# Two conditioned linear layers in fp32 on one core: y's parts from PSUM in the first batch, W0's last slabs turned by VectorE, x and these slabs loaded as eight and four row blocks

## The reference

```python
def _L0_cond_ref(hidden_states, W, b, coeff, mask):
    output = jnp.einsum('bsi,oi->bso', hidden_states, W) + b
    sign = (2 * mask - 1).astype(hidden_states.dtype)
    diff = jnp.einsum('bsi,bio->bso', hidden_states, sign)
    return output + diff * coeff[:, None, None]

def _L1_cond_ref(x, adapter_ids, base_weight, base_bias, lora_A_w, lora_B_w):
    result = jnp.einsum('bsd,od->bso', x, base_weight) + base_bias
    A = lora_A_w[adapter_ids]
    Bw = lora_B_w[adapter_ids]
    h = jnp.einsum('bsd,brd->bsr', x, A)
    lora_out = jnp.einsum('bsr,bor->bso', h, Bw)
    return result + lora_out

x = x + _L0_cond_ref(x, W0, b0, coeff, mask)
x = x + _L1_cond_ref(x, ids, W1, b1, lora_a, lora_b)
```

## Time and profile before

| what | value |
|---|---|
| runs | 408.07, 409.04, 409.2 us; median 409.04 |
| the profiled execution | 409.28 us, its span 407.5 us |
| busy of the span | PE 98%, PEld 90%, DVE 71%, ACT 45%, POOL 7% |
| granted clock of PE | full in all 40 slices |
| moved | 63.33 MB in 93488 packets, mean 155 GB/s |
| issue to landing, median | mask 4.7 us, a quarter of x 6.3 us, slab of W0 5.3 us, of W1 7.7 us |

### The profile page before, as it was taken

How to read it: one execution, slowest core, us unless ns; L and a number is a source line. 1 busy time by engine, 2 the same in 40 slices (tenths; PEclk the granted TensorE clock), 3 DMA queues, 4 the chain that set the end, 5 groups by cost and what they waited for, 6 DMA issues and landing times.

```text
span 407.5 us, 6136 instructions
## 1 busy us (share of the span) xinstructions
PE 397.8 (98%) x2356; PEld 365.3 (90%) x2356; DVE 290.6 (71%) x375; ACT 183.2 (45%) x289; POOL 26.5 (7%) x43
## 2 busy tenths in 40 slices
PE   7999989999999999999999999999999999999995
PEld 5788878889999999999999999999999999999995
DVE  2578878866887688676887679675887679775523
ACT  3565645544435344354444444354345434353322
POOL 1234510000001000010001000010001000000000
PEclk9999999999999999999999999999999999999999
DMA  7999997159532892249622893339732693346002
GB/s 267 287 272 262 246 275 189 51 144 251 161 97 74 194 244 76 80 136 238 182 82 72 197 225 97 93 120 196 189 110 77 184 238 103 104 129 168 0 2 103
DMA packets 93488, 63.33 MB, mean 155 GB/s; under 512 B 3595, under 2 KB 90643, under 8 KB 93460
## 3 DMA queue, kind: packets, MB, share of 16 engines
q1 hardware_dynamic: 93298, 62.77, 59.2%
q10 hardware_dynamic: 162, 0.18, 0.1%
HBM read 51.39 MB, written 8.39 MB: 147 GB/s over the span
## 4 chain that ended last, share of the span: by engine, by line
PE 90%; DMA 5%; SPq 3%; issue 1%; DVE 1%; ACT 0%
PE ps L946 28%; PE ps L948 14%; PE ps L997 13%; PE ps L996 13%; PE ps L995 13%; PE ps L919 3%; DMA xraw<-in_x_dram 2%; PE ps L1018 2%; DMA xrows<-in_x_dram 2%; SPq L292 1%; PE ps L975 1%; PE ps L974 1%; PE ps L973 1%; DMA araw<-in_L_cond_lora_A_w_dram 1%; SPq L261 0%
## 5 line engine op out<-in xcount | busy, mean ns | idle before, releaser
L946 PE MATMUL ps<-xhl,whi 128*128 128x512 f32 x512 | 183.9, 397 | 0.1
L948 PE MATMUL ps<-xhl,wlo 128*128 128x256 f32 x512 | 143.2, 280 | 0.0
L946 PEld LDWEIGHTS ps<-xhl,whi 128*128 128x128 f32 x512 | 96.1, 188 | 19.6 <-issue 0.5
L997 PE MATMUL ps<-w1hi,yhl 128*128 128x344 f32 (+1 forms) x336 | 107.8, 321 | 0.0
L996 PE MATMUL ps<-w1lo,yhl 128*128 128x344 f32 (+1 forms) x336 | 107.6, 320 | 0.0
L995 PE MATMUL ps<-w1hi,yhl 128*128 128x344 f32 (+1 forms) x336 | 107.5, 320 | 0.0
L948 PEld LDWEIGHTS ps<-xhl,wlo 128*128 128x128 f32 x512 | 96.6, 189 | 0.4
L707 DVE SCALAR_TENSOR_TENSOR wlo<-wm,cs_minus,whi 128x1024 fp32r<-128x1024 f32 x62 | 80.0, 1291 | 20.7 <-ACT whi L487 20.7
L487 ACT ACTIVATE whi<-wm,cs_minus 128x1024 fp32r<-128x1024 f32 x62 | 71.5, 1153 | 39.7 <-DVE wm L700 39.7
L700 DVE SCALAR_TENSOR_TENSOR wm<-wm,cs_twice,w0t 128x1024 f32<-128x1024 int32 x62 | 80.1, 1291 | 3.9 <-DMA wm<-in_mask_Bx4096x_ik_dram 2.8
L527 ACT ACTIVATE ysum<-ps,b0col 128x256 f32<-128x256 f32 x64 | 30.4, 475 | 87.2 <-PE ps L948 87.0
(11 more groups left out here) (72 smaller groups left out, 234.2 us busy)
## 6 DMA issues: line engine op xcount, KB each, us to landing
wm<-in_mask_Bx4096x_ik_dram SPq DMA_DIRECT2D x64, 512.0 KB, 4.7
xraw<-in_x_dram SPq DMA_DIRECT2D x28, 256.0 KB, 6.3
w0raw<-in_L_cond_W_dram SPq DMA_DIRECT2D x8, 512.0 KB, 5.3
w1raw<-_L_cond_base_weight_dram SPq DMA_DIRECT2D x8, 512.0 KB, 7.7
out_dram<-zst SPq DMA_DIRECT2D x18, 172.0 KB, 2.0
bt<-bhl SPq DMA_DIRECT2D x48, 64.0 KB, 2.4
out_dram<-zst SPq DMA_DIRECT2D x8, 164.0 KB, 2.0
out_dram<-zst SPq DMA_DIRECT2D x7, 176.0 KB, 2.0
```

The source lines that it names most:

```text
L946: nc.tensor.matmul(ps[:, bank, :], whi[:, s, k, :], xhl[:, b % 2, k, :], start=(k == 0), stop=False, skip_group_check=True)
L948: op = nc.tensor.matmul(ps[:, bank, 0:S], wlo[:, s, k, :], xhl[:, b % 2, k, 0:S], start=False, stop=(k == KT - 1), skip_group_check=True)
L997: op = nc.tensor.matmul(dst, lo, w1hi[:, c, cols], start=False, stop=(c == KT - 1), skip_group_check=True)
```

## The change

**(a) y in the first batch.** For n < 8 `layer1` becomes `first_layer1`: whi x xhi, whi x xlo and wlo x xhi are three matmuls of 256 columns that all add into the same 256 columns of PSUM. So `half_y` and `make_y` fall away there; `first_y_hi` (ACT) and `first_y_lo` (DVE, one scalar_tensor_tensor) read PSUM directly. yhl has three places in this part. Layer 1 of the next chunk waits for `first_y_lo`.

**(b) W0's slabs 5, 6 and 7** are loaded by four DMAs each into the layout that x has, and DVE turns them, `turn_w0`, in place of two units on PE and two copies on ACT each. POOL adds the unit matrix in that layout in one operation.

**(c) `load_x`**, for all batches, is eight DMAs of 128 partitions by 256 elements, one per block of 32 rows, in place of four.

**(d) The order of stage 1** is written anew on all engines. **(e)** `HELD` has one tile more.

```diff
+    W0D = range(5, KT)
-    HELD = ((1, 2),)
+    HELD = ((1, 1), (1, 2))
...
-                for a in range(4):
-                    src = x[b, :, a * S:(a + 1) * S].rearrange("(n q) f -> q n f", q=Q)
-                    sp.dma_start(xraw[a * Q:(a + 1) * Q, :, :], src).then_inc(x_in, 16)
+                for r in range(S // Q):
+                    src = x[b, r * Q:(r + 1) * Q, :].rearrange("q (a f) -> a q f", f=S)
+                    sp.dma_start(xraw[:, r, :], src).then_inc(x_in, 16)
...
+                if c in W0D:
+                    for r in range(P // Q):
+                        src = W0[c * P + r * Q:c * P + (r + 1) * Q, :].rearrange("q (a f) -> a q f", f=S)
+                        sp.dma_start(w0raw[:, s, r * S:(r + 1) * S], src).then_inc(w0_in[c], 16)
+                else:
+                    sp.dma_start(w0raw[:, s, :], W0[c * P:(c + 1) * P, :]).then_inc(w0_in[c], 16)
...
+            def first_y_hi(n):
+                act.wait_ge(l1_done, n + 1)
...
+                nc.scalar.activation(yhl[:, n % 3, 0:S], ps[:, l1_bank(n), 0:S], ACT.Identity,
+                                     bias=b0col[:, n:n + 1]).then_inc(y_hi, 1)
...
+            def turn_w0(c):
+                dve.wait_ge(w0_eyed, c + 1)
+                nc.vector.transpose(w0t[:, c, :, :].rearrange("p k (n q) -> p n k q", q=Q),
+                                    w0raw[:, c % W0S, :].rearrange("p (n i k) -> p n k i", n=4, k=KT)).then_inc(w0_by_dve, 1)
...
+            def first_y_lo(n):
+                dve.wait_ge(y_hi, n + 1)
+                nc.vector.scalar_tensor_tensor(yhl[:, n % 3, S:2 * S], ps[:, l1_bank(n), 0:S], b0col[:, n:n + 1],
+                                               yhl[:, n % 3, 0:S].bitcast(F32), ALU.add, ALU.subtract).then_inc(y_lo, 1)
...
+                    if not low:
+                        nc.tensor.matmul(ps[:, l1_bank(n), 0:S], whi[:, s, k, :], xhl[:, 0, k, 0:S],
+                                         start=(k == 0), stop=False, skip_group_check=True)
+                    if low is not False:
+                        op = nc.tensor.matmul(ps[:, l1_bank(n), 0:S], whi[:, s, k, :], xhl[:, 0, k, S:],
+                                              start=False, stop=(low is True and k == KT - 1), skip_group_check=True)
+                    if not low:
+                        op = nc.tensor.matmul(ps[:, l1_bank(n), 0:S], wlo[:, s, k, :], xhl[:, 0, k, 0:S],
+                                              start=False, stop=(low is None and k == KT - 1), skip_group_check=True)
```

More of the change, by code:

```diff
@@ L506, in rows_hi @@
                 if b == 1 and g == 1:
-                    act.wait_ge(unit_turned, max(number["w0", 5, 1], number["b", 0, 1]) + 1)
-                elif b == 1:
-                    act.wait_ge(unit_turned, number["w0", KT - 1, 1] + 1)
+                    act.wait_ge(unit_turned, number["b", 0, 1] + 1)
+                if b == 1:
+                    for c in (5,) if g == 1 else (6, 7):
+                        if c in W0D:
+                            act.wait_ge(w0_by_dve, c - W0D.start + 1)
+                        else:
+                            act.wait_ge(unit_turned, number["w0", c, 1] + 1)
                 if b >= 2:
@@ L696, in make_w @@
                 dve.wait_ge(mask_in[n % MS], 16 * (n // MS + 1))
-                if b == 0:
+                if b == 0 and c in W0D:
+                    dve.wait_ge(w0_by_dve, c - W0D.start + 1)
+                elif b == 0:
                     dve.wait_ge(w0_copied, 2 * (c + 1))
@@ L814, in _ @@
             split_lo("w1", 2, 1)
+            chunk_lo(3)
             split_lo("a", 0, 0)
             split_lo("a", 0, 1)
-            chunk_lo(3)
-            make_y(2)
+            first_y_lo(2)
+            turn_w0(5)
             make_w(4)
@@ L920, in turn_unit, with first_layer1 @@
                 op.then_inc(unit_turned, 1)
-            def layer1(n, ks):
-                b, c = divmod(n, KT)
-                bank = l1_bank(n)
+            def first_layer1(n, ks, low=None):
                 s = n % WS
-                if ks[0] == 0:
+                if ks[0] == 0 and not low:
                     if n < 2:
@@ L938, in layer1 @@
+                if ks[-1] == KT - 1 and low is not False:
+                    op.then_inc(l1_done, 1)
+            def layer1(n, ks):
+                b, c = divmod(n, KT)
+                bank = l1_bank(n)
+                s = n % WS
+                if ks[0] == 0:
+                    pe.wait_ge(w_lo, n + 1)
+                    if n == KT:
+                        pe.wait_ge(y_lo, KT)
+                    elif n == KT + 1:
                         pe.wait_ge(parts_lo, parted(number["w1", KT - 1, 0]))
-                    if c == 0 and b > 0:
+                    else:
+                        pe.wait_ge(y_made, n - 1 - KT)
+                    if c == 0:
@@ L1125, in _ @@
-            layer1(6, range(6, 8))
-            first_layer2(4, 1, 1)
-            adapter_h(5)
+            first_layer1(5, range(2, 4))
+            first_layer1(5, range(4, 6))
+            first_layer1(5, range(6, 8))
+            first_layer2(3, 1, 1)
+            first_layer2(4, 0, 0)
+            first_layer2(4, 1, 0)
+            adapter_h(4)
+            first_layer2(4, 0, 1)
+            first_layer1(6, range(0, 2))
+            first_layer1(6, range(2, 4))
+            first_layer1(6, range(4, 6))
@@ L1143, in _ @@
+            turn_unit("w1", 7, 0)
+            first_layer2(6, 1, 1)
+            turn_unit("w1", 7, 1)
+            adapter_h(7)
             layer1(8, range(0, 2))
```

328 lines of the change are left out of this document (156 added, 172 removed).

## The result

The changed kernel takes 458.96 us (456.75 to 459.58, 4 runs) against 409.12 us for the kernel before: 1.121 times as long, 95% interval 1.117 to 1.126. The profiled execution took 458.37 us, its span is 456.6 us, 49.1 more than before.

The account below looks back on a forecast made before the run. The prediction took PE, busy 98% of 407.5 us, as the bound, but expected the transfers to decide: 16.8 + 24.0 - 0.2 = +40.6 on the profiled 409.28, about 450 us, range 418 to 485.

Parts of the forecast that it names:

- four engines: The new x and W0 slab loads run on 4 of 16 DMA engines, their source's first count; chance 0.82.
- (a): Rival: all 16 DMA engines share the new loads as before; -3.6, 405.4 us, faster; chance 0.12.
- (b): Rival: four engines, and x's own price of 74 ns per 1 KB piece stays; about 505 us; chance 0.06.
- (c): Rival: 16 engines, but the 64 added weight loads on PE show, +13.8; 419 us; chance 0.04.
- (d): Rival: the parts cancel within 1.2 us, DVE's three turns making PE wait as long as it saves; chance 0.02.
- The engines' part: Gain with transfers at no cost: -2.64 for PE's removed transposes, -0.8 at the start, -0.2 at the end; -3.6 us.
- The price, 48 ns: Time for 1 KB on one DMA engine in the new loads; 12.3 us for x, 6.1 for a W0 slab.
- Each later batch, 4.0: x lands late, so PE waits 4.0 us for wlo in each of six batches, x(2) to x(7): +24.0.
- (e): Rival: with four engines PE waits 5 to 9 us at a time and runs slower afterwards; 6 more, 456 us.
- the factor of 1.6: PE work after a long wait takes up to 1.6 times as long, over some 10 us.
- Stage 1, +16.8: x(1) lands at about 80.2, not 53.3, so chunk 9's layer 1 begins at 100.0, not 83.23; bounds +8 and +26.
- Lie inside that wait and count nothing: Stage 1: the engines' gains there are hidden in PE's wait for the late loads and add 0.

Follow-up runs that it names:

- the 16-partition run: The changed kernel with W0's slabs in the 32-partition shape and x in eight DMAs of 16 partitions by 8 by 256: 413.41 us, ratio 1.006.

## Why the prediction was right, and where its terms were off

The forecast was 450 us for 458.96, by four engines, which was given 0.82, and the rivals fell: (a) 405.4 is what the same change takes when the loads do use 16 engines (405.78 measured); (b) fell with the price of a piece; (c) with the kernel of both old loads at 405.78, not 419; (d) with it.

- **The engines' part**, -3.6: measured -3.9 (405.78 against 409.64), and -4.7 with x in eight DMAs. Right in sum. The end's -0.2 is hardly seen (about 0.1), in stage 1 there is a little more. The -2.64 for the transposes and the -0.8 for the start were not tried one by one. The 64 added weight loads show in PE's timeline of the changed kernel:

```profile
63.22 0.28 PE L973 MATMUL ps<-xhl,whi 128*128 128x256 f32 x1
63.34 0.28 PE L976 MATMUL ps<-xhl,whi 128*128 128x256 f32 x1
63.46 0.28 PE L979 MATMUL ps<-xhl,wlo 128*128 128x256 f32 x1
63.58 0.40 PE L1026 MATMUL ps<-w1hi,yhl 128*128 128x512 f32 x1
```

Three products of 256 columns take 63.58 - 63.22 = 0.36, where 0.352 was the pace before: 64 x 0.008 = 0.5 us, near the 0 that was taken and far from 13.8.
- **Four engines**: share 0.27 and 96 GB/s, against "near a quarter" and "near 85". The step that a trace of before could not show, and the page of the Trainium skill did (DMA: Bandwidth & Descriptors, section "Why a DMA increments its semaphore by 16 and not by 1"); the runs with 2 and 8 as first counts agree with it.
- **The price, 48 ns**: alone, a piece takes 43 ns. But from the time at which x(2) could begin (about 106 us, when the rate falls to 96) to the turn at 118.23 it is 12.2 us, 48 ns a piece: towards the end the masks issued behind it move at the same time (217 GB/s from 112 to 114 us) and pass through the same engines. The sum's 12.3 was right for a reason that it did not have: luck.
- **Each later batch, 4.0**: the waits are 3.6 to 5.2 us, 25.0 / 6 = 4.2 in the mean. Right. What the sum lacked is the clock behind the wait: 2.1 us in each batch, 12.4 in all. This is the largest error: a stall of 4 us costs 6 here. The prediction had the clock as rival (e), but for waits of 5 to 9 us, which it looked for in stage 1, and priced it at 6 in all. Its 456 is near the 458.96 by luck: the steady part alone lost twice that, while stage 1 lost less than forecast. Nor does the factor of 1.6 come from rows at a lower clock: the eight transposes of 1.97 us ran at the full one (1.00 from 6.80 to 11.00). At 0.50 the pace is half.
- **Stage 1, +16.8**: measured +11.7, between the bounds of 8 and 26. x(1) was turned at 73.86, where it was to land at 80.2. The step that failed there is the addition of shared and unshared loads end to end at a mean rate of 265 GB/s. The sum had 30.7 us of four-engine transfer; the windows of stage 1 at 0.27 to 0.35, where nearly nothing else moved, are 28 to 30, 44 to 50 and 60 to 68, 16 us in all. Two of them:

```profile
46.00:48.00 2.00, 2.00 (x15) 1.87 (x16) 1.97 (x2) 1.17 (x2) 0.00 (x0) 1.00 0.27 96
```

```profile
66.00:68.00 2.00, 2.00 (x16) 1.87 (x15) 0.61 (x1) 0.00 (x0) 0.00 (x0) 1.00 0.27 97
```

The rest went beside shared loads. How the 6.3 us between 80.2 and 73.86 split is not shown.
- "Lie inside that wait and count nothing", said of the engines' gains in stage 1, was wrong. Against the kernel with the same plan and shared loads (chunk 9 at 80.08) the new loads cost stage 1 14.9, near the 16.8; the other 3.2 is what the plan gained. Two runs say the same: with the new x load and shared W0 slabs in both, the new order starts chunk 9 at 85.90, the old one at 89.81. The old order with all the new loads was not tried.

So 16.8 + 24.0 was forecast and 11.7 + 37.4 came: two errors of +5.1 and -13.4 which partly cancel, and without that luck the forecast would have been further off.

## What to carry to other kernels

Look at the outermost count of both sides of every large DMA, not at the number of partitions that it fills: a rearrangement that puts a 4 in front ran at a quarter of the engines here (a share of 0.27), although it filled all 128 partitions of SBUF. A transfer that no engine waits for has a slack that can be read from the trace; here it was 2.5 us, and one load that became 7 us longer used it up in each of six batches. Count a stall of some us on a saturated PE as more than its length (25.0 us of waits cost 37.4). A change of this kind can be saved by its parts: the same re-plan with the two loads in their old shape is the fastest kernel of this study, 404.2 us with x in eight DMAs, 1.2% less than before.

## What was not expected of the hardware

- The number of engines alone did not give the rate of 1 KB pieces: 220 GB/s for 32 partitions at a time on 16 engines, 140 for 16 on 16, 85 for 8 on eight, while 128 partitions took 96 GB/s from four engines. Eight engines on 8 partitions were slower than four on 128. Whether the partitions or the order of the pieces is the cause stays open.
- The six waits of 3.6 to 5.2 us in the changed kernel each came with a stretch of PE at half its clock, 3.4 us long in four batches and 6.8 in two. The length of the wait did not tell which: 3.76 us went with 6.8, 4.78 with 3.4. The four waits of the 16-partition run, 1.7 us at most, left it full (its mean clock is 1.00).
